# A token tower on one core: joint rows of normed input and base for the last five expert blocks, fixed positions for the experts' first blocks, and one opening per PSUM bank

## The reference

```python
def _L0_ffn_ref(x, gate_w, w1, w2, w3, sw1, sw2):
    ...
    E = 8
    K = 1
    D = 128
    I = 512
    ...
    xf = x.reshape(-1, D)
    logits = xf @ gate_w.T
    wts, idx = jax.lax.top_k(logits, K)
    wts = jax.nn.softmax(wts, axis=-1)
    comb = jnp.einsum('nke,nk->ne', jax.nn.one_hot(idx, E, dtype=xf.dtype), wts)
    h = jax.nn.silu(jnp.einsum('nd,eid->nei', xf, w1)) * jnp.einsum('nd,eid->nei', xf, w3)
    y = jnp.einsum('nei,edi->nd', h * comb[:, :, None], w2)
    y = y + jax.nn.gelu(xf @ sw1.T, approximate=False) @ sw2.T
    return y.reshape(x.shape)
...
h = _L0_tok_ref(x, L0_tok_W)
h = h + _L0_attn_ref(_layernorm(h, axis=-1), ...)
h = h + _L0_ffn_ref(_layernorm(h, axis=-1), ...)
```

## Time and profile before

| | |
|---|---|
| median of 3 runs | 178.74 us (178.38 to 179.56) |
| the profiled execution | 178.78 us |
| its span, first to last instruction | 177.0 us |
| TensorE busy | 137.2 us (78%), 989 matmuls |
| TensorE weight loads | 100.6 us (57%) |
| VectorE busy | 125.1 us (71%) |
| ScalarE busy | 102.5 us (58%) |
| GpSimd busy | 83.8 us (47%), 77 instructions |
| TensorE clock granted | 1.0 of full speed until the last 9 us, 0.5 there |

### The profile page before, as it was taken

One profiled execution on the slowest core, in us unless ns is written; L12 is line 12 of the kernel. 1 busy time (PEld: TensorE's weight loads), 2 busy tenths in 40 slices (PEclk: granted clock), 3 DMA queues, 4 the chain that ended last, 5 costly groups with the idle time before them and its releaser, 6 DMA issues. The chain is left out here.

```text
span 177.0 us, 3209 instructions
## 1 busy us (share of the span) xinstructions
PE 137.2 (78%) x989; PEld 100.6 (57%) x989; DVE 125.1 (71%) x362; ACT 102.5 (58%) x237; POOL 83.8 (47%) x77
## 2 busy tenths in 40 slices
PE   0104997778898888888599999879999999999510
PEld 0103875556666656677354698647667766666300
DVE  1245585947499985799968839668888888887610
ACT  2000454499989993476878993437565766564200
POOL 3767873910000000143300278740877778788760
PEclk9999999999999999999999999999999999999955
DMA  5565345999000000011110024150232244353340
GB/s 131 175 185 143 104 107 163 313 394 397 22 0 0 4 0 4 0 63 59 59 63 0 0 61 146 49 163 4 32 47 48 30 50 41 33 47 36 31 46 0
DMA packets 9955, 14.37 MB, mean 81 GB/s; under 512 B 1936, under 2 KB 4624, under 8 KB 9936
## 3 DMA queue, kind: packets, MB, share of 16 engines
q1 hardware_dynamic: 5904, 10.45, 17.2%
q0 software_dynamic: 4032, 3.67, 14.0%
HBM read 10.71 MB, written 3.41 MB: 80 GB/s over the span
## 5 line engine op out<-in xcount | busy, mean ns | idle before, releaser
L431 POOL DMA_INDIRECT out<-w_sb,row_of x20 | 31.4, 1572 | 11.9 <-DVE w_sb L1234 7.3
L484 PE MATMUL bank<-states,sq_sb 128*128 128x128 f32 x112 | 27.3, 327 | 6.5 <-ACT states L726 1.2
L658 PE MATMUL bank<-w_hl,xblk_t 128*128 x120 | 29.2, 379 | 0.3 <-issue 0.3
L412 POOL TENSOR_TENSOR rstd<-vareps,cst 128x2 f32<-128x2 f32 x8 | 5.7, 709 | 45.8 <-DVE vareps L877 45.8
L484 PEld LDWEIGHTS bank<-states,sq_sb 128*128 128x128 f32 x112 | 17.6, 198 | 15.0 <-ACT states L726 14.7
L482 PE MATMUL bank<-x_in,sq_sb 128*128 128x128 f32 x112 | 23.5, 292 | 1.6 <-ACT x_in L719 1.5
L726 ACT ACTIVATE states<-bank 128x128 f32<-128x128 f32 x56 | 15.5, 276 | 12.3 <-PE bank L484 12.1
L836 ACT ACTIVATE w_sb<-bank,factor 128x512 f32<-128x512 f32 x20 | 13.7, 687 | 13.0 <-PE bank L658 12.9
L424 POOL DMA_INDIRECT w_sb<-x_rows,row_in x16 | 18.0, 1122 | 4.9 <-issue 4.9
L482 PEld LDWEIGHTS bank<-x_in,sq_sb 128*128 128x128 f32 x112 | 18.1, 202 | 2.7 <-ACT x_in L719 1.6
L380 POOL DMA_INDIRECT emb_rows<-emb,tok_sb x16 | 15.6, 972 | 6.5 <-issue 4.3
(11 more groups left out here) (162 smaller groups left out, 278.5 us busy)
## 6 DMA issues: line engine op xcount, KB each, us to landing
w_sb<-w SPq DMA_DIRECT2D x24, 256.0 KB, 5.8
x_rows<-norm SPq DMA_DIRECT2D x4, 256.0 KB, 2.4
out<-attn_out SPq DMA_DIRECT2D x4, 256.0 KB, 2.7
late<-places SPq DMA_DIRECT2D x1, 619.5 KB, 7.0
sw_sb<-sw SPq DMA_DIRECT2D x2, 256.0 KB, 2.9
cst<-consts SPq DMA_DIRECT2D x1, 420.0 KB, 3.8
sq_sb<-sq SPq DMA_DIRECT2D x1, 384.0 KB, 3.9
out<-w_sb,row_of POOLq DMA_INDIRECT x20, 3.4
```

The lines of the kernel that those rows point to most:

```text
L431: pool.indirect_dma_start(out=out, out_offset=bass.IndirectOffsetOnAxis(ap=row_of[:, k:k + 1], axis=0), in_=out_blk[k % OUTS], in_offset=N ...
L484: pe.matmul(pre, at, states[:, i * COLS:(i + 1) * COLS], start=False, stop=True).then_inc(pre_ready, 1)
L658: mm = pe.matmul(hb[:], xblk_t[:, k % 3, b * P:(b + 1) * P], w[:, bass.ds(e * INNER + a * EXPERTS * INNER, INNER)], start=(j == 0), stop=( ...
```

## The change

- `own_expert(k)`: the 20 blocks are put in another order. Positions 0 to 11 (`OWN_FROM`) hold the experts' further blocks, whose expert is only known at run time, and positions 12 to 19 hold the first block of expert 0 to 7. Each expert now has a first block, if empty. Since the expert of positions 12 to 19 is fixed, their weights stand at fixed addresses, and the two operands change places: 24 matmuls of 128 columns with the weights stationary give the product transposed already. The four transposes of `prod` are left out for them, the high and low halves are taken from `prod` in SBUF, and the second product is 12 matmuls of 128 columns into `turned`, whose two banks alternate, in place of bank 6. VectorE's `out_part` is left out for them.
- `with_base(k)`: SyncE stores `norm2` and the base a second time, side by side into rows of 1024 bytes (`x_base`): eight more DMAs of 256 KB. Blocks 15 to 19 gather these joint rows, add the base on VectorE, and are scattered plainly (`bypass`), without the add. `AHEAD` goes from 12 to 15.
- The matmuls of zeros are left out; the first matmul into each bank opens it.
- `turn_block(2)` moves ahead of `block_ups(1)`, `take_down(3)` into VectorE's step 0, and `take_down(0)` and `take_down(1)` behind later parts. All 20 blocks run without a branch, which comes behind them. The routing chain computes `lane_nth` without integer steps, gets the expert of a block (`past`, `owned`) on its way, and makes `lane_hot` in two halves.

The diff, cut to its core:

```diff
--- before.py
+++ after.py
...
-SLOTS = 20
-AHEAD = 12
+BESIDE_BASE = ((1, 11), (1, 13), (0, 0), (0, 2), (1, 0))
+AHEAD = 15
...
+SPREAD = BLOCKS - EXPERTS
+OWN_FROM = FEW - EXPERTS
...
+        def with_base(k):
+
+            return AHEAD <= k < FEW
+
+        def slot(k):
+
+            if with_base(k):
+                under, v = BESIDE_BASE[k - AHEAD]
+                return (xblk_under if under else xblk_beside)[:, v:v + 2, :]
+            v = k if k < AHEAD else k - FEW + 6
+            return xblk_beside[:, v, :] if v < BESIDE else xblk_under[:, v - BESIDE, :]
+
+        def turns_to_free(k):
+
+            if with_base(k):
+                under, v = BESIDE_BASE[k - AHEAD]
+                return 0 if under and v + BESIDE >= AHEAD else v + 2 + under * BESIDE
+            return 0 if k < AHEAD else k - FEW + 7
...
-        def pipelined(eng, body, lag, few):
-
-            for k in range(FEW - 2):
-                body(k, k % RING, k, BLOCKS)
-            for is_few, end in ((0, BLOCKS), (1, FEW)):
-                with eng.If(few == is_few):
-                    for k in range(FEW - 2, end + lag):
-                        body(k, k % RING, k, end)
+        def pipelined(eng, body, lag):
+
+            for k in range(FEW + lag):
+                body(k, 0, FEW)
+            few = load_few(eng)
+            with eng.If(few == 0):
+                for k in range(FEW - 2, BLOCKS + lag):
+                    body(k, FEW, BLOCKS)
...
+        def own_expert(k):
+
+            return k - OWN_FROM if OWN_FROM <= k < OWN_FROM + EXPERTS else None
+
+        def column(k):
+
+            return EXPERTS + k if k < OWN_FROM else k - OWN_FROM if k < OWN_FROM + EXPERTS else k
+
+        def turns_up_to(k):
+
+            return k + 1 - min(max(k + 1 - OWN_FROM, 0), EXPERTS)
...
+                sp.dma_start(per_tile(x_base[:, 0:P], g), norm2[:, 4 * g:4 * g + 4, :]).then_inc(joined, 16)
+            for g in range(GROUPS):
                 sp.wait_ge(base_ready, g + 1)
                 sp.dma_start(per_tile(out[0:ROWS, :], g), attn_out[:, 4 * g:4 * g + 4, :]).then_inc(base_stored, 16)
+                sp.dma_start(per_tile(x_base[:, P:2 * P], g), attn_out[:, 4 * g:4 * g + 4, :]).then_inc(joined, 16)
...
-                if k >= SLOTS:
-                    pool.wait_ge(blk_turned, k - SLOTS + 1)
-                pool.indirect_dma_start(out=xblk(k), out_offset=None, in_=x_rows,
-                                        in_offset=bass.IndirectOffsetOnAxis(ap=row_in[:, k:k + 1], axis=0),
+                if turns_to_free(k):
+                    pool.wait_ge(blk_turned, turns_to_free(k))
+                rows = x_rows
+                if with_base(k):
+                    pool.wait_ge(joined, 16 * 2 * GROUPS)
+                    rows = x_base
+                pool.indirect_dma_start(out=slot(k).rearrange("q h d -> q (h d)") if with_base(k) else slot(k),
+                                        out_offset=None, in_=rows,
+                                        in_offset=bass.IndirectOffsetOnAxis(ap=row_in[:, column(k):column(k) + 1], axis=0),
                                         ).then_inc(xblk_in[k], 16)
 
             def add_block(k):
 
                 pool.wait_ge(outb_ready, k + 1)
-                pool.indirect_dma_start(out=out, out_offset=bass.IndirectOffsetOnAxis(ap=row_of[:, k:k + 1], axis=0),
-                                        in_=out_blk[k % OUTS], in_offset=None, compute_op=ALU.add
+                pool.indirect_dma_start(out=out, out_offset=bass.IndirectOffsetOnAxis(ap=row_of[:, column(k):column(k) + 1], axis=0),
+                                        in_=out_blk[k % OUTS], in_offset=None,
+                                        compute_op=ALU.bypass if with_base(k) else ALU.add
...
-                if i == 0:
-                    pe.matmul(down_bank[g][:], zeros[:], zeros[:, 0:1].to_broadcast([P, GC]), start=True, stop=False)
...
+                                       sw2_sb[:, i * P:(i + 1) * P], start=(i == 0 and t == 0), stop=(i == IC - 1 and t == 3))
...
-            pe.wait_ge(hots_ready, 1)
             for t in range(TILES):
+                if t % (TILES // 2) == 0:
+                    pe.wait_ge(hots_ready, 1 + t // (TILES // 2))
...
+                    if own is not None:
+                        for i in range(IC):
+                            at_i = own * INNER + i * P
+                            for j, (a, b) in enumerate(halves):
+                                mm = pe.matmul(hb[:, i * P:(i + 1) * P], w_hl[:, a, at_i:at_i + P],
+                                               xblk_t[:, k % 3, b * P:(b + 1) * P], start=(j == 0), stop=(j == 2))
+                        mm.then_inc(h_done, 1)
+                        continue
...
-                    few = load_few(pe)
...
+            turn_block(2)
             block_ups(1)
...
+                if live(-2) and k >= 1:
                     turn_block(k + 2)
-                if live(1):
+                if live(1) and own_expert(k - 1) is None:
                     pe.wait_ge(prod_ready, k)
-                    if k >= 3:
+                    if k >= 3 and own_expert(k - 3) is not None:
+                        pe.wait_ge(outb_ready, k - 2)
+                    elif k >= 3:
                         pe.wait_ge(prod_low, k - 2)
                     else:
                         pe.wait_ge(base_ready, k + 2)
                     for i in range(IC):
                         mm = pe.transpose(turned[1 - u][:, i * P:(i + 1) * P], prod[:, 1 - u, i * P:(i + 1) * P], ident)
                     mm.then_inc(prod_turned, 1)
-                if live(2):
-                    e2 = pe.snap(expert_of[(v - 2) % RING], min_val=0, max_val=EXPERTS - 1)
+                if live(2) and own_expert(k - 2) is not None:
+                    own = own_expert(k - 2)
                     pe.wait_ge(prod_low, k - 1)
-                    if static is None or static >= 3:
+                    if k >= 4 and own_expert(k - 4) is not None:
+                        pe.wait_ge(outb_ready, k - 3)
+                    elif k < 4:
+                        pe.wait_ge(base_ready, k + 1)
+                    for i in range(IC):
+                        for j, (a, b) in enumerate(((0, 0), (1, 0), (0, 1)) if i == 0 else ((1, 0), (0, 1), (0, 0))):
+                            mm = pe.matmul(turned[u][:, 0:P], (prod_hi, prod_lo)[a][:, u, i * P:(i + 1) * P],
+                                           w2_hl[:, own * IC + i, b, :],
+                                           start=(i == 0 and j == 0), stop=(i == IC - 1 and j == 2))
+                    mm.then_inc(y_done, 1)
...
+                    own = own_expert(k - 1)
+                    if own is None:
+                        act.wait_ge(prod_turned, turns_up_to(k - 1))
+                    else:
+                        act.wait_ge(prod_ready, k)
+                    if k >= 3:
                         act.wait_ge(y_done, k - 2)
-                    act.activation(prod_hi[:, 1 - u, :], turned[1 - u][:], ACT.Copy).then_inc(prod_high, 1)
+                    act.activation(prod_hi[:, 1 - u, :], turned[1 - u][:] if own is None else prod[:, 1 - u, :], ACT.Copy
...
+            dve.tensor_reduce(owned[:], d_e(past[:]), AX.X, ALU.add)
...
-            then_wait(dve.tensor_copy(slot_i[:], slot_f[:]))
-            dve.tensor_scalar(lane_nth_i[:, 0, :], slot_i[:], P - 1, None, ALU.bitwise_and)
-            then_wait(dve.tensor_scalar(lane_nth_i[:, 1, :], slot_i[:], 7, None, ALU.logical_shift_right))
-            then_wait(dve.tensor_copy(lane_nth[:], lane_nth_i[:]))
+            dve.tensor_copy(nth_of[:, 0:EXPERTS], blocks_start[:])
+            then_wait(dve.tensor_scalar(slot_down[:], slot_f[:], -(P - 1) / 2, WHOLE_BLOCKS, ALU.add, ALU.add))
+            dve.scalar_tensor_tensor(out=lane_nth[:, 0, :], in0=slot_down[:], scalar=WHOLE_BLOCKS, in1=slot_f[:],
+                                     op0=ALU.subtract, op1=ALU.subtract)
+            then_wait(dve.tensor_scalar(lane_nth[:, 1, :], slot_down[:], WHOLE_BLOCKS, 1.0 / P, ALU.subtract, ALU.mult))
...
+            for h in range(2):
+                ts = slice(h * TILES // 2, (h + 1) * TILES // 2)
+                dve.tensor_tensor(lane_hot[:, :, ts], lanes[:, :, ts],
+                                  lane_nth[:, 0:1, ts].to_broadcast([P, P, TILES // 2]), ALU.is_equal
+                                  ).then_inc(hots_ready, 1)
...
-                if n == 10:
+                if n == 9:
+                    take_down(0)
+                if n == 11:
                     take_down(1)
...
-            take_down(3)
...
+                if k == 0:
+                    take_down(3)
...
+                    if with_base(k - 2):
+                        dve.wait_ge(xblk_in[k - 2], 16)
+                        dve.scalar_tensor_tensor(out=out_part[:, u, :], in0=bank[6][:, P:2 * P], scalar=y_unscale,
```

(12 more changed lines are left out.)

124 lines of the change are left out of this document (67 added, 57 removed).

## The result

The changed kernel takes 173.09 us (median of 4 executions, 172.80 to 173.84) beside 178.92 us for the kernel before (178.38 to 179.56) on the same chip: a ratio of 0.968, interval 0.963 to 0.973. The forecast was 170.5, its range 168.2 to 174.2; so the change brings 5.8 us where 8.3 were forecast. The profiled execution took 172.8 us, with a span of 170.7.

What follows compares the result with a forecast made beforehand. TensorE's chain was taken to set the end, with GpSimd just behind it. From 178.78 us, 7.95 on TensorE's path and 0.7 of landing came off and 0.4 of contention was added: 170.5 us, range 168.2 to 174.2.

Steps and rivals of the forecast that it cites:

- openings and register loads: TensorE before the steps: four matmuls of zeros left out, 0.9 us, and one of three register loads gone, 0.3 us.
- first steps: TensorE from block 1's product to the steps' own: two waits go, 3.24 us becomes 1.95, a gain of 1.3 us.
- from there to block 19's product: TensorE's fixed-expert blocks: no transposes, 2.11 us a step, and the branch off its path; a gain of 2.75 us.
- the end: From block 19's product to VectorE's result: no bank 6 wait, transposes or `out_part`; a gain of 2.7 us, low end 2.1.
- the third rival: 128-column matmuls with large weights run slower than L613's: 175.7 to 180.9 us, or 177.8 at 81 ns; chance 0.04.
- the fourth rival: TensorE's clock falls in the fixed blocks because it waits in each step: 17 us given back, 187 us; chance 0.03.
- spare time of the chain: Fixed blocks: the low half has 5.67 us from its block's first product, the last took 4.40; about 1 us to spare.
- GpSimd's sum: GpSimd's queue: gathers end at 121.8, then five pairs, ten scatters, four plain starts; last scatter at 161.5, level with TensorE.
- landing: At the very end: a plain scatter lands like a gather, 0.7 us less than a scatter-add, between 0 and 0.9.
- hold-ups: GpSimd contending with VectorE instructions that have two SBUF inputs: half of one 0.74 us hold-up charged, 0.4 us.
- The first rival: GpSimd becomes the bound, by plain scatters priced like adds or stretched gathers and pairs: 171.9 to 174.1, around 173; chance 0.22.
- The eight stores: SyncE's extra stores for the joint rows: hidden by the steps before the first joint gather, about 125 us; no cost.

Runs made afterwards that it cites:

- e1: The changed kernel with up to eight gathers in flight on GpSimd in place of three; 171.61 us, ratio 0.951 to the kernel before.
- e9: The changed kernel without the eight stores to `x_base`; last five blocks gather from `x_rows`, base from wrong rows in SBUF; 173.77 us, ratio 0.976.
- e4: The changed kernel with twelve gathers ahead of the first scatter and eight alternating with the scatters; 174.84 us, ratio 0.971.

## Why the prediction was right in TensorE and short in GpSimd

**TensorE's sum held.** The last result came 7.89 us sooner, 7.95 were forecast. By parts: up to block 1's product 1.27 (openings and register loads, 1.2 forecast), first steps 1.40 (1.3), from there to block 19's product 2.46 (2.75), the end 2.76 (2.7). First steps: from block 1's product to the next step's 116.14 - 114.30 = 1.84 us, 3.24 before and 1.95 forecast, without a wait. Pace of fixed blocks: 2.12 for 2.11. 128-column matmuls with large weights: 24 in 1.34 us, 0.056 each, as L613's, so the third rival falls. By the 81 ns of the Trainium skill (page "TensorE: Matmul & The Clock Gate", section "Back-to-back issue gap") they would have taken 1.94 us, an estimate from the page's figure; this trace disagrees. The granted clock stayed at 1.00 through the fixed blocks (in each 5 us from 140 to 160); the fourth rival did not come. At the end 5.15 us stood for the 5.2 forecast. The spare time of the chain was less than "about 1 us". VectorE's low half of block 16,

```profile
154.89 0.69 DVE L1313 TENSOR_TENSOR w_sb<-w_sb 128x512 f16<-128x512 f32 x1
```

was complete at 155.58, 5.30 us after the start of its block's first product (150.28), where the prediction took 4.40 from the last block; the second product started at 155.87, so 0.3 us were left.

**The step that failed in GpSimd's sum** is "three more at 1.25 each (0.94 + 0.30) end at 121.8". The gathers were priced at their issue, as the twelve before had shown it; that each may start only when the third before it has landed was no term, because in the kernel before no gather ever waited for that. It had little reserve: a gather is issued every 1.25 us, three make 3.75, and landings went up to 4.6. That one, the fifth, did no harm in the kernel before because the gathers behind it were themselves held up (2.11 and 1.68 us to issue), so that the eighth came 5.65 us after it. In the changed kernel landings reached 6.1, at the twelfth gather, which there is a block of 14 tokens and in the kernel before was one of 128; the new order of the blocks is part of the change. So the first scatter came 2.6 us late, and GpSimd, which the forecast had level with TensorE, carried this unchanged to the end: 124.39 + 16.0 (five pairs) + 18.8 (ten scatters, 18.5 forecast) + 5.25 (four plain starts, 5.16) = 164.46. The profiled execution adds up: 170.5 + 2.56 (last scatter 164.46 for 161.9) - 0.2 (landing 0.9 for 0.7) - 0.4 (hold-ups, charged beforehand, now within the 2.56) + 0.32 (outside the span) = 172.8.

The first rival had the right engine and the right time (173), but neither of its two mechanisms made it: the plain scatter had the low price, and what made the gathers late was not their issue but their landing. So it is luck that the range, drawn to that rival's far end, held the time. e1 is the changed kernel without the waits: 0.951 x 178.92 = 170.2 us as an estimate from its ratio, 173.09 - 1.7 = 171.4 from the positions; the forecast's 170.5 lies between.

A second term was missing, and e1 shows it: the forecast let the last scatter follow the last result by the 0.28 us of the kernel before, where the last two results stand 2.25 us apart. Without a wait for bank 6 they come 0.86 us apart, less than the 1.27 of two scatters, and in e1 the last scatter follows by 1.06 us. That is 0.8 us, which no limit on the gathers gives back.

**The eight stores**, costed at nothing, cost nothing that e9 shows. My explanation after the first result, that they held the gathers back, was wrong; what made the landings long is open between the rows that the gathers read, the stores to `out`, which are in both kernels, and the two together.

**Landing:** forecast 0.7 less, measured 0.90 at the tail and 1.1 to 1.2 in the landing (2.2 for 3.3 to 3.4), beyond the bound of 0.9. **Hold-ups:** 0.4 forecast; in the changed kernel the scatters beside the low half took 1.70 and 1.59 for 1.55 and 1.14 for 0.98, 0.35 in all; in e4, with more backlog, several took 1.8 and one 2.03, and its chain (20.29 + 8 x 3.2 + 7 x 1.86 + 4 x 1.27 = 64.0, measured 65.58) lost some 1.6 us.

## What to carry to other kernels

When a queue's work is moved up or lengthened, price it by its landings too: a limit of n transfers in flight is harmless only while the slowest landing is under n issues, and the trace shows how near it is before anything waits. An engine that was "just behind" the bound before may be the bound after, as GpSimd was here: make its own sum from the first instruction, with each wait it could meet. Where several results of one chain come close together at the end, the queue behind them drains at its own pace (e1). And when an explanation rests on added traffic, take the traffic away wholly (e9) before refining it.
